# The first mixture's combination, LN2, the network's dense product and its first rows in one block, by groups of 500 tokens

## The reference, cut to what matters

```
x = x + gnn0(layernorm(x))                      # edge-weighted sums
x = x + moe0(layernorm(x))                      # 8 experts, the best 2 of each token
    # out = tokens; for each expert e: out = out + combine[:, e] * (gelu(tokens @ w1[e] + b1[e]) @ w2[e] + b2[e])
x = x + gnn1(layernorm(x), ...)                 # h = xn @ W_in + b_in; three layers:
    # pooled = segment_sum(edge_weight * h[src], dst) + h;  hid = relu(bn(pooled @ W1[l] + b1[l]));
    # h = relu(bn(hid @ W2[l] + b2[l]))
x = x + moe1(layernorm(x))                      # 8 experts of width 1024, and a shared one
```

## Time and profile before

| what | value |
|---|---|
| median of 3 runs | 3071.66 us (3067.74 to 3076.16) |
| the profiled execution | 3069.2 us, of which the span from first to last instruction is 3067.4 us |
| PE busy | 2369.1 us, 77% of the span |
| POOL busy | 1483.2 us, 48% |
| DVE busy | 1367.9 us, 45% |
| ACT busy | 919.8 us, 30% |
| mean granted TensorE clock | 0.876 |

### The profile page before, as it was taken

One profiled execution on the slowest core, in us unless ns is written; L12 is line 12 of the kernel. 1 busy time (PEld: TensorE's weight loads), 2 busy tenths in 40 slices (PEclk: granted clock), 3 DMA queues, 4 the chain that ended last, 5 costly groups with the idle time before them and its releaser, 6 DMA issues. The chain is left out here.

```text
span 3067.4 us, 52751 instructions
## 1 busy us (share of the span) xinstructions
PE 2369.1 (77%) x14132; PEld 2129.8 (69%) x14132; DVE 1367.9 (45%) x3807; ACT 919.8 (30%) x2699; POOL 1483.2 (48%) x1446
## 2 busy tenths in 40 slices
PE   1989959999868707777665776567775699999999
PEld 0789958888767604666545766446765499999988
DVE  6689986656443243344343443333433631111122
ACT  4258867877112201000030000220000423333332
POOL 1388867777004361777715777327776001111152
PEclk9799989999959958888778888789887789999999
DMA  2100013333028832333313333223333149999932
GB/s 77 37 4 3 3 45 100 104 104 103 6 70 292 281 91 59 106 105 105 105 24 109 105 104 104 57 76 104 104 104 98 30 146 310 329 325 328 325 86 63
DMA packets 250253, 363.12 MB, mean 118 GB/s; under 512 B 64005, under 2 KB 195554, under 8 KB 249754
## 3 DMA queue, kind: packets, MB, share of 16 engines
q0 software_dynamic: 73728, 163.66, 19.7%
q1 hardware_dynamic: 173160, 194.83, 19.4%
q10 hardware_dynamic: 3250, 3.20, 0.3%
HBM read 322.19 MB, written 38.64 MB: 118 GB/s over the span
## 5 line engine op out<-in xcount | busy, mean ns | idle before, releaser
L810 POOL DMA_INDIRECT z_or_xn<-h_rows,agg_idx x768 | 730.8, 952 | 345.4 <-issue 222.9
L841 PE MATMUL ps<-z_or_xn 128*128 128x125 f32 x3072 | 480.9, 321 | 278.9 <-DMA z_or_xn<-h_rows,agg_idx 243.0
L841 PEld LDWEIGHTS ps<-z_or_xn 128*128 128x128 f32 x3072 | 448.2, 231 | 316.0 <-issue 253.7
L1419 POOL DMA_INDIRECT moe_room<-h_rows,moe_inverse x112 | 106.1, 947 | 699.4 <-PE ps L1500 392.7
L868 DVE TENSOR_TENSOR h_features<-h_features,ps 128x250 f32 x384 | 159.2, 415 | 506.5 <-PE ps L841 457.7
L783 ACT CAST agg_idx<-slots 128x4 int32 x264 | 51.8, 196 | 1075.1 <-PE ps L841 566.2
L635 POOL DMA_INDIRECT payloads<-pay_st,idx_st x176 | 246.8, 1402 | 159.9 <-DMA idx_st<-slot_i 106.6
L810 POOL DMA_INDIRECT agg_room<-h_rows,agg_idx x256 | 250.0, 977 | 97.1 <-issue 71.1
L1619 ACT ACTIVATE moe_room<-ps,moe_b 128x128 f32<-128x128 f32 x560 | 163.1, 367 | 365.9 <-PE ps L1512 365.9
L849 DVE TENSOR_SCALAR z_or_xn<-col,agg_key 128x125 f32<-128x125 f32 x792 | 241.1, 367 | 32.2 <-ACT agg_key L784 32.2
L503 PE MATMUL ps<-perm_tile,perm_weighted 125*128 125x296 f32 x1792 | 246.4, 300 | 9.9 <-ACT perm_weighted L490 9.9
(11 more groups left out here) (272 smaller groups left out, 3708.6 us busy)
## 6 DMA issues: line engine op xcount, KB each, us to landing
moe_w_ring<-in_L_ffn_W1p_dram SPq DMA_DIRECT2D x38, 1024.0 KB, 7.3
moe_w_ring<-in_L_ffn_W2p_dram SPq DMA_DIRECT2D x38, 1024.0 KB, 7.8
moe_w_ring<-in_L_ffn_w_dram SPq DMA_DIRECT2D x76, 256.0 KB, 5.1
moe_room<-in_L_ffn_W1p_dram SPq DMA_DIRECT2D x18, 1024.0 KB, 7.2
moe_room<-in_L_ffn_W2p_dram SPq DMA_DIRECT2D x18, 1024.0 KB, 7.9
expert_out<-moe_room SPq DMA_DIRECT2D x112, 128.0 KB, 7.1
z_or_xn<-h_rows,agg_idx POOLq DMA_INDIRECT x768, 2.7
moe_room<-in_L_ffn_w_dram SPq DMA_DIRECT2D x36, 256.0 KB, 4.8
```

The lines of the kernel that those rows point to most:

```text
L810: self.pg.nc.gpsimd.indirect_dma_start(self.G[:, k, :], None, self.pg.H, bass.IndirectOffsetOnAxis(ap=self.idx[:, k:k + 1], axis=0)).then_ ...
L841: last = nc.tensor.matmul(out[:, c, :], self.G[:, k, c * 128:(c + 1) * 128], self.S[:, k, :], start=(u == 0), stop=(u == PAIR - 1))
```

## The change

The combination's loop moves into one pipeline with what the next block of code did, and that block is gone:

- The network's weights, vectors and the features `h` (`net.h`) become an object, `Network`, that lives from before the first mixture. SP issues its 14 loads in the mixture, between the router's and the biases'. The one-hot matrices of the mixture's sorting (`place1`) and its transposed rows lie in `net.h`.
- The tokens run in seven groups (six of 4 blocks, one of 1 block). DVE combines a group's blocks, takes their statistics and makes LN2's numbers for this group alone; ACT (no longer DVE) normalises, copies the transposed blocks out of PSUM into two buffers, evacuates the product and copies the first rows. PE transposes group c, multiplies it by `W_in`, and then makes the first rows of group c-1.
- Gathered rows land in `XN` and in `rows`, which hold all 25 blocks; a gather waits for a combination only 13 blocks back (`RB`). `rows` lies in the mixture's working room, whose weights and tiles are no longer used by then.
- SP stores each block's first rows by itself: 25 stores of 125 rows instead of 5 of 625.
- The accumulator of the first aggregation is zeroed there, on DVE behind its first eight one-hot matrices, instead of on POOL in the removed block.

The core of the diff (moved code and buffer layout cut):

```diff
-        self.W = sb("w_ring", [128, self.RW - 1, 4 * F])
+        self.w_ring = at["w"].rearrange("p (r f) -> p r f", r=self.RW)
-            self.xnt = at["xnt"].rearrange("p (k n) -> p k n", k=KD)
+            self.xnt = net.h
+            self.rows = room[0:P, 0:NT * D].rearrange("p (j d) -> p j d", j=NT)
+            self.features = self.b2_sb[:].rearrange("p e d -> p (e d)")[:, 0:2 * KD * CH].rearrange(
+                "p (r k n) -> p r k n", r=2, k=KD)
...
+            if self.net:
+                self.net.load(sp)
             small(self.b1_sb[:], self.b1.rearrange("e (k p) -> p e k", p=128), self.s_w)
...
+        if self.net:
+            for j in range(NT):
+                sp.wait_ge(self.s_ro, j + 1)
+                sp.dma_start(pg.H[j * P:(j + 1) * P, :], self.rows[:, j, :]).then_inc(self.s_rst, 16)
+            sp.wait_ge(self.s_rst, 16 * NT)
...
+            for j in range(NT):
+                r = j % self.RB
+                if j >= self.RB:
+                    pool.wait_ge(self.s_comb, j - self.RB + 1)
+                for c in range(TOP):
+                    g.indirect_dma_start((self.rows if c else self.XN)[:, j, :], None, pg.Y, bass.IndirectOffsetOnAxis(
+                        ap=self.slot_i[:, c * NT + j:c * NT + j + 1], axis=0)).then_inc(self.s_back[r].sem, 16)
...
+    def net_scalar(self, act):
+        def rows(c, j0, n):
+            for j in range(j0, j0 + n):
+                act.wait_ge(self.s_r, j + 1)
+                a.copy(self.rows[:, j, :], ps[0:P, 6 + j % 2, 0:D]).then_inc(self.s_ro, 1)
...
+        for c, j0, n in self.groups:
+            js = slice(j0, j0 + n)
+            act.wait_ge(self.s_sum, c + 1)
+            a.activation(self.rstd[:, js], self.var[:, js], ACT.Sqrt).then_inc(self.s_root, 1)
+            act.wait_ge(self.s_shift, c + 1)
+            for j in range(j0, j0 + n):
+                a.activation(self.XN[:, j, :], self.pg.X[:, j, :], ACT.Identity, bias=self.shift[:, j:j + 1],
+                             scale=self.rstd[:, j:j + 1]).then_inc(self.s_n, 1)
...
+            for j in range(j0, j0 + n):
+                act.wait_ge(self.s_nt, j + 1)
+                a.copy(self.features[:, c % 2, :, (j - j0) * P:(j - j0 + 1) * P],
+                       ps[:, j % 2, 0:256].rearrange("p (k q) -> p k q", k=KD)[:, :, 0:P]).then_inc(self.s_nf, 1)
+            for fo in range(KD):
+                act.wait_ge(self.s_p, c * KD + fo + 1)
+                a.activation(net.h[:, fo, j0 * P:(j0 + n) * P], self.net_psum(c, fo, n), ACT.Identity,
+                             bias=net.bi[:, fo:fo + 1]).then_inc(self.s_h, 1)
+            if c:
+                rows(*self.groups[c - 1])
+        rows(*self.groups[-1])
...
+                if clear:
+                    nc.vector.memset(acc[:], 0.0).then_inc(s_zero, 1)
+                    dve.wait_ge(s_zero, 1)
```

More of the change, by code:

```diff
@@ L1103, in stage_aggregate_features @@
         Hh = pg.sb(f"{tag}_hot_rows", [P, HOT, D], ctx=ctx)
-        s_ld, s_mm, s_add, s_tick = (pg.sem(f"{tag}_share_{n}", ctx) for n in ("rows", "mm", "add", "tick"))
+        s_ld, s_mm, s_add, s_tick, s_zero = (pg.sem(f"{tag}_share_{n}", ctx) for n in (
+            "rows", "mm", "add", "tick", "zeroed"))
         def product(pe, c, first, width):
@@ L1247, in __init__ @@
         self.y = at["y"].rearrange("p (r d) -> p r d", r=self.RY)
-        self.g = at["g"][0:P].rearrange("p (r c d) -> p r c d", r=self.RG, c=TOP)
-        self.w_last = at["w_last"]
+        late, wide = (self.RW - 1) * 4 * F, self.COLS * 128
         if shared:
@@ L1276, in __init__ @@
         count = lambda n, r, ring: 16 * ((n - r + ring - 1) // ring)
-        arrived = pg.arrivals(self.RX + self.RG, [count(self.T, r, self.RX) for r in range(self.RX)]
-                              + [TOP * count(NT, r, self.RG) for r in range(self.RG)])
+        back = self.RG if shared else self.RB
+        arrived = pg.arrivals(self.RX + back, [count(self.T, r, self.RX) for r in range(self.RX)]
+                              + [TOP * count(NT, r, back) for r in range(back)])
         self.s_got, self.s_back = arrived[:self.RX], arrived[self.RX:]
@@ L1562, in tensor, with net_tensor, transposes, product @@
             shared_fc2(len(SHARED_CHUNKS) - 1)
+        if self.net:
+            self.net_tensor(pe)
+    def net_tensor(self, pe):
+        nc, ps, net, G = self.pg.nc, self.pg.ps, self.net, len(self.groups)
+        def transposes(j0, n):
+            for j in range(j0, j0 + n):
+                pe.wait_ge(self.s_n, j + 1)
+                if j >= 2:
+                    pe.wait_ge(self.s_nf, j - 1)
+                for k in range(KD):
+                    last = nc.tensor.transpose(ps[:, j % 2, k * 128:k * 128 + P],
+                                               self.XN[:, j, k * 128:(k + 1) * 128], self.pg.ident[0:P, 0:P])
+                last.then_inc(self.s_nt, 1)
+        def product(c, j0, n):
+            pe.wait_ge(self.s_nf, j0 + n)
+            for fo in range(KD):
+                if c >= 2:
+                    pe.wait_ge(self.s_h, (c - 2) * KD + fo + 1)
+                for k in range(KD):
+                    last = nc.tensor.matmul(self.net_psum(c, fo, n), net.W[:, 0, k, fo * 128:(fo + 1) * 128],
+                                            self.features[:, c % 2, k, 0:n * P], start=(k == 0), stop=(k == KD - 1))
+                last.then_inc(self.s_p, 1)
+        def rows(c, j0, n):
+            pe.wait_ge(self.s_h, (c + 1) * KD)
+            for j in range(j0, j0 + n):
+                if j >= 2:
+                    pe.wait_ge(self.s_ro, j - 1)
+                for k in range(KD):
+                    last = nc.tensor.matmul(ps[0:P, 6 + j % 2, 0:D], net.h[:, k, j * P:(j + 1) * P], net.W[:, 1, k, :],
+                                            start=(k == 0), stop=(k == KD - 1))
+                last.then_inc(self.s_r, 1)
+        pe.wait_ge(net.s_w, net.loads)
+        pe.wait_ge(self.s_y, self.T)
+        for c, j0, n in self.groups:
+            transposes(j0, n)
+            product(c, j0, n)
+            if c:
+                rows(*self.groups[c - 1])
+        rows(*self.groups[G - 1])
+    def net_psum(self, c, fo, n):
+        return self.pg.ps[:, 2 + 2 * (c % 2) + fo, 0:n * P]
     def shared_psum(self, j):
@@ L1687, in vector @@
                 ins.then_inc(self.s_comb, 1)
-                if self.out is None:
-                    row_stats(pg, dve, j, self.s_comb)
-                elif j not in late:
+                if j not in late:
                     dve.wait_ge(self.s_comb, n + 1)
```

226 lines of the change are left out of this document (103 added, 123 removed).

## The result

The changed kernel takes 3023.66 us (median of 4 runs, 3020.94 to 3026.06) where the kernel before, beside it, took 3072.61. The ratio is 0.9846 with a 95% interval of 0.9835 to 0.9858: 1.5% faster. The profiled execution took 3022.26 us against 3069.2, with a span of 3020.5 against 3067.4, 46.9 us less.

A forecast was written before the change was run, and what follows sets the result against it. The prediction took one engine working at a time, from 1063 to 1221 us, as the bound here. The profiled 3069.2 us less 49.9 gives 3019.3; with the median 2.5 above, it put 3021, range 3008 to 3042.

The forecast's parts named there:

- the forecast's own case: Whole kernel: groups of 12.5 to 14 us, time 3014 to 3028 us; chance 68%.
- the stretch: From the first gather of expert rows to the load of the hot rows: 49.9 us gained, load at 1171.3 instead of 1221.15.
- Gathers and group 0: Start of pipeline: gathers unchanged at 12.2 us a group, group 0's variance ready at 1081.4, ACT free of it at 1095.0.
- The pace, 13.1 a group: Groups 1 to 5 on ACT and PE: 13.1 us each, halfway between the gathers' 12.2 and 14.0 at clock 0.78.
- Who waits: Roots on ACT: 12 to 14 us apart, from the third on later than DVE's variance.
- The tail, 8.3: Group 6's root to last copy: one block's chain, then five blocks of first rows, 8.3 us, ending at 1168.8.
- The last store, 2.5: End of block: issue 0.5 us, landing 1.7, barrier 0.3, up to the hot rows' load at 1171.3.
- Elsewhere, 0: First mixture and aggregation: 14 loads hidden, router's weights and memset cost 0, each bounded by 2 us.
- the clock stays up: Rival: product and rows hold 2.4 GHz from group 1, gathers bound; 56 us gained, 3013 or 3016 us; 12%.
- the clock stays at half speed: Rival: clock falls in each pause, stays at 1.2 GHz, groups of 19.3 us; 14 us gained, 3055 or 3058; 10%.
- No overlap: Rival: queue order makes groups wait for the next gathers, dense work follows all gathers; 7 us lost, 3076 us; 5%.
- taking turns: Rival: PE and ACT work in sequence at 1.2 GHz, from 24 us a group slower by 9 us or more, 3081; 5%.

The follow-up runs named there:

- seven extra matmuls: Changed kernel plus seven useless matmuls a group on PE, before, between and behind the group's transposes: 3019.90 us, 0.9844 of the kernel before.
- the split load: Changed kernel with stores, and also the hot rows' load, split by partitions in the same way: 3018.30 us, 0.9832 of the kernel before.
- the order: Changed kernel with a group's first rows behind its own product, interleaved with the next group's transposes: 3014.76 us, 0.9817 of the kernel before.
- four extra matmuls: Changed kernel plus four useless matmuls a group, three before the first transpose and one between third and fourth: 3023.06 us, 0.9838 of the kernel before.

## Why the prediction was right, point by point

The forecast was 3021 us (the sum as written gives 3021.8); the median is 3023.66, inside the range and inside the narrower range of the forecast's own case. The profiled execution took 3.0 us more than the sum's 3019.3: 1.3 in the stretch, which gave 48.6 us and not 49.9, and 2.26 from the shift ahead of the change, less 0.5 behind the load. Set 2.26 us later, as the stretch was, its steps stand against the trace like this:

- **Gathers and group 0.** Variance of group 0 ready at 1081.4 + 2.26 = 1083.7: the trace has 1083.8. ACT free of group 0 at 1097.3: the root of group 1 starts at 1096.56, 0.7 us sooner, most of it since the first product was at half clock for most of its length only (6.15 us instead of 6.7).
- **The pace, 13.1 a group.** Measured 13.07 (groups 1 to 6). It was taken halfway between 12.2 and 14.0 on the thought that product and rows run denser than the mean clock of 0.78 says. The size was right and the split was not: the clock does not lie between its levels for both, the product pays nearly all (4.98 us instead of the 3.62 of a product at full clock) and the rows nothing (3.62 in every group). Against that the hand-overs were shorter than costed: root to normalising 0.65 for 0.8, normalising and transposes up to the product 3.61 (1114.79 - 1111.18) for 4.0. For group 2: 0.65 + 3.61 + 5.15 from product to first rows + 3.92 for rows and last copy = 13.33. The chain at full clock is 11.64 us (group 3) and not 12.1, and the clock adds 1.4 on average and not 1.0. The two misses, 0.5 and 0.4 us, cancel, so that 13.07 came so near 13.1 is in part luck. Group 3 also shows that a group can go below 12.2, the gathers having run ahead of the chain by then.
- **Who waits.** "From the third on later than DVE's variance": DVE's waits of 2.52 us and more from group 2 on, with 1.05 at group 4, whose forerunner had the one quick product.
- **The tail, 8.3.** From the root of group 6 at 1161.90 to the end of the last copy, 1170.02: 8.1.
- **The last store, 2.5.** Here is the one term that was clearly off: 4.76. The prediction priced one store by the quickest landing of a store of 128 rows, 1.7 us, and let the stores before it lie beside other work. Stores of 125 partitions move 90 to 116 KB a microsecond, so one takes more time than the 0.86 us in which the next block's rows are made; the last few queue. Split, they take 2.34, near the price that was forecast. The other terms of the stretch took 1.0 us back (0.7 from group 0, 0.2 from the tail, 0.1 from five groups), which leaves the gain at 48.6 instead of 49.9.
- **Elsewhere, 0.** The 14 loads took SP from 845.76 to 855.95, 10.2 us for the forecast's 10; the stores of normalised rows end at 880.8 and SP's load for the owners follows at 896.49, so they are hidden. PE's first transposes of the mixture stand at 848.41, later than before by the shift that the whole mixture has. For the memset the forecast left 1.3 us of slack; the row shows 0.03, because it starts 1.25 us behind the one-hots. The cost was still 0.04 us, but it is the split load that shows how near the edge this lies.

The rivals: that the clock stays up needed groups of 12.2 bound by gathers; seven extra matmuls make nearly that kernel (12.0 from group 2 on, where DVE still waits up to 1.0 us for the root, so chain and gathers are about level), and it isn't this one. That the clock stays at half speed needed groups of 19.3; the rule of the Trainium skill that speaks for it ("TensorE: Matmul & The Clock Gate", section "HAM oscillation — how this bites in real kernels": bursts cut by waits start at half clock each time) agrees with this trace in part: four products in five of groups 1 to 5 were at half clock from their start or within 0.6 us of it. But the clock returns before each of these products ends, so it costs 1.4 us a group (4.98 for 3.62 in the product) and not 7: that every burst would stay at half clock to its end was the rival's reading, and the trace does not bear it out. No overlap and taking turns are excluded by the table of stretches.

## What to carry to other kernels

When stages are laid over each other, write down the serial chain of one step, engine by engine in the order of its queues, beside the pace of its supply, and look at which of the two waits at the hand-over: the one that doesn't wait is the one to shorten, and shortening the other gives little (gathers 12.5 us sooner, 3.6 us gained). The clock is a term of that chain: filling the thin stretch ahead of a dense burst with other useful work (the order, which also shortened the chain) gained 8.65 us, filling it with work of no use 4.9. And the last store of a block is on the path, so look at how many DMA engines its shape uses.

## What the runs showed of the hardware

- An indirect gather of 125 rows holds POOL for 1.18 to 1.21 us, one of 128 rows for 0.94 to 0.95; start to start 1.51 to 1.53 against 1.26 to 1.28.
- Stores of 125 partitions keep the DMA engines 0.33 busy and move 90 to 116 KB a microsecond; the same rows as 112 and 13 keep them 0.55 busy at 163 KB a microsecond and shorten the end of the block from 4.76 to 2.34 us.
- Around a thin stretch of transposes the changed kernel's granted clock fell from 1.00 to 0.50 anywhere from 2.9 us before the dense product behind it to 0.6 us after its start (in one group of five not at all), and was back before the product ended. It fell with four extra matmuls in that stretch as without any; with seven it stayed up from group 2 on.
- The same pipeline of groups, run four times, took 102.7 to 106.1 us from first gather to last copy. In three of them one product in groups 1 to 5, each time that of group 3, kept the full clock, in the slowest none did; no run shows why.
